# Spreading the value rows of a linear recurrence by DMA copies instead of selection matmuls

## The reference, cut to what matters

```
def step(s, rkvw):                                  # per head: s is 16 x 16 (i, j)
    r_t, k_t, v_t, w_t = rkvw
    bonus = jnp.exp(u + k_t)[..., :, None] * v_t[..., None, :]
    o_t = jnp.einsum('bhi,bhij->bhj', r_t, s + bonus)
    s = jnp.exp(w_t)[..., None] * s + k_t[..., :, None] * v_t[..., None, :]
    return (s, o_t)
```

## Time and profile before

| | |
|---|---|
| three runs | 2797.94, 2774.63, 2772.53 us; median 2774.63 us |
| profiled execution | 2782.58 us, span 2780.8 us |
| busy: PE, weight load, DVE, ACT, POOL | 2181.0 (78%), 1573.9 (57%), 1731.5 (62%), 917.0 (33%), 597.4 (21%) us |
| mean granted clock of TensorE | 0.845 |
| DMA | 34.34 MB in all, queue share 3.8% of 16 engines' span |

### The profile page before, as it was taken

How to read it: one execution, slowest core, us unless ns; L and a number is a source line. 1 busy time by engine, 2 the same in 40 slices (tenths; PEclk the granted TensorE clock), 3 DMA queues, 4 the chain that set the end, 5 groups by cost and what they waited for, 6 DMA issues and landing times. The chain is left out here.

```text
span 2780.8 us, 30306 instructions
## 1 busy us (share of the span) xinstructions
PE 2181.0 (78%) x10060; PEld 1573.9 (57%) x10060; DVE 1731.5 (62%) x3123; ACT 917.0 (33%) x2186; POOL 597.4 (21%) x357
## 2 busy tenths in 40 slices
PE   0885996796787698688678769965519999999998
PEld 0683574474465457447446645742117777777775
DVE  3335686578668668657866866866726554555544
ACT  0342452343344245234334424531004222222232
POOL 0000133033223213303322321331421011110110
PEclk9756897878888789788888878977559999999999
DMA  4000000000000000000000000000022000000000
GB/s 127 1 1 8 1 1 8 8 1 8 9 1 1 16 1 1 8 9 1 8 9 1 1 16 1 1 1 8 0 61 69 16 13 4 15 15 15 15 0 16
DMA packets 32435, 34.34 MB, mean 12 GB/s; under 512 B 4512, under 2 KB 31200, under 8 KB 31968
## 3 DMA queue, kind: packets, MB, share of 16 engines
q1 hardware_dynamic: 32288, 32.43, 3.8%
HBM read 24.04 MB, written 8.39 MB: 12 GB/s over the span
## 5 line engine op out<-in xcount | busy, mean ns | idle before, releaser
L563 DVE TENSOR_TENSOR_SCAN s_buf<-r_work,kvb 128x512 f32<-128x512 f32 x256 | 337.3, 1320 | 0.0
L719 ACT ACTIVATE probs<-bank,nmx 128x256 f32<-128x256 f32 (+1 forms) x512 | 224.4, 445 | 265.8 <-DVE nmx L425 265.5
L990 PEld LDWEIGHTS bank<-v_tok,pt 128*128 128x128 f32 x1792 | 265.3, 218 | 14.9 <-issue 3.4
L990 PE MATMUL bank<-v_tok,pt 128*128 128x16 f32 x1792 | 252.3, 272 | 2.2 <-DVE work L449 2.2
L552 DVE TENSOR_TENSOR kvb<-r_work,bank 128x512 f32<-128x512 f32 x256 | 174.3, 683 | 115.8 <-PE bank L1089 110.2
L661 POOL TENSOR_TENSOR r_work<-s_buf,r_work 128x512 f32<-128x512 f32 x128 | 157.7, 1232 | 335.0 <-DVE s_buf L563 335.0
L1544 PE MATMUL mbank<-m_xh,w_hi 128*128 128x512 f32 x544 | 228.6, 420 | 0.4 <-issue 0.3
L1352 DVE TENSOR_TENSOR hl<-hf,hh 128x512 fp32r<-128x512 f32 x136 | 94.0, 691 | 200.0 <-ACT hh L1459 199.5
L1544 PE MATMUL mbank<-m_xl,w_hi 128*128 128x512 f32 x544 | 215.5, 396 | 0.0
L1544 PE MATMUL mbank<-m_xh,w_lo 128*128 128x512 f32 x544 | 215.5, 396 | 0.0
L661 POOL TENSOR_TENSOR p_buf<-s_buf,r_work 128x512 f32<-128x512 f32 x128 | 151.4, 1183 | 291.0 <-DVE s_buf L563 284.4
(11 more groups left out here) (247 smaller groups left out, 4515.0 us busy)
## 6 DMA issues: line engine op xcount, KB each, us to landing
w_raw<-in_w SPq DMA_DIRECT2D x17, 256.0 KB, 2.7
x_new<-in_x SPq DMA_DIRECT2D x8, 512.0 KB, 3.5
x_after_rwkv<-x_b SPq DMA_DIRECT2D x8, 512.0 KB, 3.3
m_x_tok<-x_after_rwkv SPq DMA_DIRECT2D x8, 512.0 KB, 3.9
out<-m_x_tok SPq DMA_DIRECT2D x8, 512.0 KB, 2.9
w_raw<-in_w2e SPq DMA_DIRECT2D x17, 128.0 KB, 2.6
work<-in_w SPq DMA_DIRECT2D x2, 1024.0 KB
wrk<-in_wrk SPq DMA_DIRECT2D x1, 1024.0 KB
```

The lines of the kernel that those rows point to most:

```text
L563: V.tensor_tensor_scan(s_buf[:, n % 2, 1:S + 1], dec[:, n // HD, :], kvb[:, n % 2, :], 0.0, ALU.mult, ALU.add).then_inc(sem["state"], 1)
L719: ins = A(probs[:, i, h * w:h * w + w], bank[n % 2][:, h * w:h * w + w], ACT.Exp, bias=nmx[:, n, h:h + 1], accum_out=rsum[:, i, 2 * p + h: ...
L990: ins = T.matmul(A3[:, 32 * i + 16 * h:32 * i + 16 * h + 16], pt[:, m % 2, (h * len(blocks) + c) * P:(h * len(blocks) + c + 1) * P], v_tok ...
```

## The change

The values stay float32 in one SBUF tile `v_f`; `v_hi`, `v_lo`, `sel_v`, its loads and cast, and the spreading matmuls are gone. SP issues one DMA for each step, 32 in a batch, from the 8 rows of `v_f` onto the 128 rows of one of four slots of `v_bc`: each row of 2 KB is read 16 times. The DMA of step n waits until `kv(n-4)` has freed its slot. `kv(n)` now waits for its DMA, reads both inputs from SBUF, and writes into PSUM bank R0 or R1; the scan reads that bank instead of `kvb`.

```diff
+VSLOTS = 4
...
-        v_hi = sb("v_hi", [P, NK, S], F32R)
-        v_lo = sb("v_lo", [P, NK, S], F32R)
-        kvb = sb("kvb", [P, 2, S])
+        v_f = sb("v_f", [P, NK, S])
+        v_bc = sb("v_bc", [P, VSLOTS, S])
...
-            sel_rows = t["c_selv"].rearrange("(h j) n -> j h n", j=HD)
-            for j in range(HD):
-                load(raw[8 * j:8 * j + 8, 4096:6144], sel_rows[j])
...
+            def spread_v(b):
+
+                for n in range(N_SCAN):
+                    g, j, slot = n // HD, row_of(n), n % VSLOTS
+                    if n == 0:
+                        sp.wait_ge(sem["v_f"], at(b, "v_f", 2))
+                    if n >= VSLOTS:
+                        sp.wait_ge(sem["kv"], at(b, "kv", n - VSLOTS + 1))
+                    sp.dma_start(v_bc[:, slot, :], bc(v_f[8 * j:8 * j + 8, g, :].unsqueeze(1), 8, HD, S)
+                                 ).then_inc(sem[f"v_bc{slot}"], 16)
+
             next_x(0)
             with sp.Fori(1, B - 1) as b:
+                spread_v(b - 1)
                 next_x(b)
                 store(b - 1)
+            spread_v(B - 2)
             store(B - 2)
+            spread_v(B - 1)
             store(B - 1)
...
-            V.tensor_copy(sel_v[:].rearrange("p a m -> p (a m)"), raw[:, 4096:6144])
...
-                    ins = V.tensor_tensor(v_lo[:, g, :], vf[:, g, :], v_hi[:, g, :].bitcast(F32), ALU.subtract)
-                ins.then_inc(sem["v_lo"], 1)
...
                 def kv(n):
-                    ve.wait_ge(sem["v_bc"], at(b, "v_bc", n + 1))
+                    landed = f"v_bc{n % VSLOTS}"
+                    ve.wait_ge(sem[landed], at(b, landed, 16 * (n // VSLOTS + 1)))
                     if n >= 2:
                         ve.wait_ge(sem["state"], at(b, "state", n - 1))
-                    V.tensor_tensor(kvb[:, n % 2, :], kf[:, n // HD, :], RB[n % 2][:], ALU.mult).then_inc(sem["kv"], 1)
+                    if n == 1:
+                        ve.wait_ge(sem["bonus"], at(b, "bonus", 1))
+                    V.tensor_tensor(RB[n % 2][:], kf[:, n // HD, :], v_bc[:, n % VSLOTS, :], ALU.mult).then_inc(sem["kv"], 1)
...
-                        V.tensor_tensor_scan(s_buf[:, n % 2, 1:S + 1], dec[:, n // HD, :], kvb[:, n % 2, :], 0.0, ALU.mult, ALU.add
+                        V.tensor_tensor_scan(s_buf[:, n % 2, 1:S + 1], dec[:, n // HD, :], RB[n % 2][:], 0.0, ALU.mult, ALU.add
...
-                    A(v_hi[:, g, :], RB[(2 + g) % 3][:], ACT.Copy)
-                    A(vf[:, g, :], RB[(2 + g) % 3][:], ACT.Copy).then_inc(sem["v_f"], 1)
+                    A(v_f[:, g, :], RB[(2 + g) % 3][:], ACT.Copy).then_inc(sem["v_f"], 1)
...
-                def spread_v(n):
-                    g, j = n // HD, row_of(n)
-                    if n >= 2:
-                        pe.wait_ge(sem["kv"], at(b, "kv", n - 1))
-                    T.matmul(RB[n % 2][:], sel_v[:, j, :], v_hi[:, g, :], start=True, stop=False)
-                    T.matmul(RB[n % 2][:], sel_v[:, j, :], v_lo[:, g, :], start=False, stop=True).then_inc(sem["v_bc"], 1)
-
-                pe.wait_ge(sem["v_lo"], at(b, "v_lo", 1))
-                spread_v(0)
-                pe.wait_ge(sem["bonus"], at(b, "bonus", 1))
-                spread_v(1)
...
-                    if n + 2 < N_SCAN:
-                        spread_v(n + 2)
```

More of the change, by code:

```diff
@@ L38 @@
     f_lo=1, h_ps=NF, g_hi=NF, g_lo=NF, f_y=NF, fy_sb=2, fy_tok=1,
-    r_var=2, r_rstd=2, r_normed=NT, r_turned=NK, r_xt=NK, mix=8, proj=8, v_f=2, v_lo=1, k_f=2, dec=2, decay=1, r_f=2,
-    rb=1, bonus_ps=1, bonus=1, v_bc=2 * HD, kv=2 * HD, state=2 * HD, rs=2 * HD, summed=8, o_sb=2, o_tok=1, o_diff=1, o_sq=1,
+    r_var=2, r_rstd=2, r_normed=NT, r_turned=NK, r_xt=NK, mix=8, proj=8, v_f=2, k_f=2, dec=2, decay=1, r_f=2,
+    rb=1, bonus_ps=1, bonus=1, v_bc0=128, v_bc1=128, v_bc2=128, v_bc3=128, kv=2 * HD, state=2 * HD, rs=2 * HD, summed=8, o_sb=2, o_tok=1, o_diff=1, o_sq=1,
     o_var=1, o_rstd=1, o_norm=1, o_back=1, o_aff=2, y_in=1, w_ps=1, x_final=1, x_out=16, own_b=3, own_c=6, x_kept=1,
@@ L135, in mid_token_layers @@
         headones = sb("headones", [P, P])
-        sel_v = sb("sel_v", [P, HD, P], F32R)
         sel_qk = sb("sel_qk", [P, PAIRS, 4, P], F32R)
@@ L527, in rwkv_head @@
                     yield f"rmix{w}"
-                vf, kf, ek, dec, rf = (r_work[:, i:i + 2, :] for i in (0, 2, 4, 6, 8))
-                for g in range(2):
-                    ve.wait_ge(sem["v_f"], at(b, "v_f", g + 1))
-                    ins = V.tensor_tensor(v_lo[:, g, :], vf[:, g, :], v_hi[:, g, :].bitcast(F32), ALU.subtract)
-                ins.then_inc(sem["v_lo"], 1)
+                kf, ek, dec, rf = (r_work[:, i:i + 2, :] for i in (2, 4, 6, 8))
                 yield "rproj0"
@@ L543, in rwkv_head @@
                 for g, src in enumerate((R1, R2)):
-                    ins = V.tensor_tensor(o_f[:, g, :], vf[:, g, :], src[:], ALU.mult)
+                    ins = V.tensor_tensor(o_f[:, g, :], v_f[:, g, :], src[:], ALU.mult)
                 ins.then_inc(sem["bonus"], 1)
```

## The result

| | before | after |
|---|---|---|
| median of 4 runs | 2779.39 us | 2875.57 us |
| profiled execution | 2782.58 us | 2874.54 us, span 2872.7 |
| mean granted clock | 0.845 | 0.792 |
| product L552 (now L560), mean ns | 683 | 920 |
| scan L563 (now L571), mean ns | 1320 | 1210 |

After to before is 1.0318, 95% interval 1.0244 to 1.0393: slower by 3.2%, where the forecast was 9%, but inside its range of 2745 to 3105 us.

A forecast was written before the change was run, and what follows sets the result against it. The prediction took DVE to bound the scan phase before, and the copies, at 4.8 us each, after: 2782.6 + 192 (woven batches) + 66 (last batch) - 10 (setup) = 3031, or 3023 us by the median; range 2745 to 3105 us.

The forecast's parts named there:

- a tenth of it lost to PE: Woven scan phase before the change: DVE's, with 12.2 us in 11 waits for PE's spreading matmul.
- A copy alone: Service time T of one 256 KB copy from 8 neighbouring rows: 4.8 us, half of 110 GB/s; ends 1.2 and 4.8.
- T = 4.8 for every copy: Woven batches: copies land every 4.8 us, copy 28 at 122.2 us against 94.8; +27.4 us each, +192 over 7.
- Rival 3: Copies at T = 3.9 us: woven batches +5 us each, last batch +40, total 2847 or 2839 us; chance 0.10.
- the wide range: Total time, 8 in 10: 2745 to 3105 us, made to take in rival 3 and rival 1.
- rival 1: Copies hidden, product collides with POOL: last-batch steps 2.9 us, +18; woven batches -2 each; 2777 or 2769 us; chance 0.17.
- What the change frees is then worth nothing: Woven batches: PE's 30.0 us, the 12.2 us of waits and scan-POOL collisions all lie under the copy wait.
- The last batch: Last batch, recurrence alone: product 31 at 136.6 us after product 0, against 71.0; +66 us.
- The setup: Start of the kernel: without the loads and cast of `sel_v`, -10 us; ends -1 and -11.
- Operands in PSUM: DVE product writing PSUM and scan reading it: 0 extra for both, at most 0.1 us a step, under the copy.
- Rival 2: Copies hidden, product beats POOL: woven batches gain 14 us, last-batch steps 1.96 us; 2663 or 2655 us; 0.13 with rival 4.
- Rival 4: Idler PE gets a lower clock, returning up to 12 us a woven batch of rival 2's gain; 2747 or 2739; 0.13 together.

The follow-up runs named there:

- experiment 2: Changed kernel without all copies but the first four, product's second input read from the PSUM bank it writes: 2734.9 us, 0.989 of before.
- experiment 4: Changed kernel, same computation, with source rows taken in the order 0, 64, 32, 96 instead of 0, 32, 64, 96: 2806.4 us, 1.015 of before.
- experiment 9: Changed kernel with every copy reading 8 neighbouring rows among rows 0 to 63 only, so values of other channels: 2974.3 us, 1.073 of before.
- experiment 3: Changed kernel with each copy's 8 source rows 4 apart instead of neighbouring, so values of other heads: 2808.8 us, 1.017 of before.
- experiment 10: Experiment 1 with one more wait, always already met, ahead of every product: 2810.6 us, 1.014 of before.
- experiment 1: Changed kernel without all copies but the first four of the first batch; products reread those four slots without waiting: 2777.8 us, 1.004 of before.
- experiment 7: Changed kernel, whole computation, with source rows stored 4 apart and product n+2 directly behind scan n: 2745.9 us, 0.989 of before.
- experiment 5: Experiment 4 with two more 512-column matmuls in each attention step, their output overwritten: 2802.3 us, 1.011 of before.
- experiment 8: Experiment 7 with two more 512-column matmuls in each attention step: 2733.4 us, 0.986 of before.

## Why the prediction was right, and where it was wrong

**What bounds the kernel: right for the copies, wrong for PE.** DVE's own steps and waits set the pace of the scan phase, and a supplier slower than they are is felt at once. But "a tenth of it lost to PE" was no reserve: with the 12.2 us of waits gone, DVE waits for attention's matmuls instead (experiment 2).

**A copy alone: right.** Half the rate of the two groups that `sel_v`'s loads showed, 4.8 us, is what one copy takes: 51 to 53 GB/s. "Reading should suffer there as writing does" held. The figure itself owes something to luck. The 110 GB/s give the whole stretch to `sel_v`, but 199 GB/s over 10 us are 1.99 MB, and `sel_v` has 1.05 of them. With the other 0.94 MB at 373 GB/s the same working gives 3.5 us a copy, an estimate from the earlier trace rows, where 4.9 was measured. The Trainium skill, "SBUF — State Buffer" (Door 1: The DMA port swizzle), has partition bit 5 leave the port unchanged, and bit 6 and bits 4 to 2 change it; experiments 4 and 9 agree, 9.9 and 236.3 us of waits, but neither separates the page's ports from other groupings of the same rows.

**T = 4.8 for every copy: this step failed.** "copy 28 is 24 copies later: 7.0 + 24 x 4.8" took the copies as strictly one behind the other, although the working of T itself had read from the earlier trace rows that successive transfers on different groups are served together. The order of rows, 0, 32, 64, 96, was in the code, and half of the successors are on other groups. From product 4, at 1983.5 us, to product 31, at 2088.6, the real mean is 105.1 / 27 = 3.9 us. By the prediction's own 203 copies that is 0.9 x 203 = 183 us less: 2848 instead of 3031. Rival 3 had this T and this time (2847), but only as two halves that don't slow each other fully, not from the order of the rows, and with one chance in ten. The forecast's own range, T from 4.4 to 5.2 or 2942 to 3104 us, misses the measured 2876; it lies in the wide range because that was stretched to take in rivals 1 and 3.

**"What the change frees is then worth nothing": right, but it hid a cost.** At T = 3.9 a woven batch should grow by 5 us (rival 3's working), counting copies alone. It grew by 11.3, and that is the second thing that the sum missed. The 6.3 us over, 44 in seven batches, less the 17.7 us by which the first batch is shorter, are the 27 us between rival 3's 2847 and the measured 2874.5. The prediction had collisions of product and POOL, but only inside rival 1, as if the copies' waits would cover them. They don't: the wait of a woven batch is in pieces (12 waits, 16.0 us, in 778.8 to 903.5), and between them DVE is the bound. Product 0 to 28 of the third woven batch, before and then after, and the waits after:

```profile
789.10:883.90 94.80, 83.93 (x540) 68.84 (x541) 77.71 (x109) 48.37 (x164) 30.82 (x27) 0.91 0.00 1
```

```profile
778.80:881.50 102.70, 85.36 (x465) 69.32 (x473) 82.36 (x109) 47.65 (x163) 31.42 (x27) 0.72 0.44 66
```

```profile
DVE bank L560 <- DMA v_bc<-v_f: 16.0, 12, 2.5
```

The stretch is 7.9 us longer. DVE is 4.6 us longer busy (its product takes 920 instead of 683 ns there, its scan less than before) and waits 3.8 us longer for values, 16.0 instead of 12.2; its other waits are the same 4 to 5 us. So in this stretch the part above rival 3's 5 us is the collisions. Other batches at a clock of 0.63 to 0.68 took up to 111.3 us for it, with longer waits for attention's matmuls; how much of the batches' mean the lower clock makes isn't settled.

**The last batch:** forecast +66, measured +42, against rival 3's +40 at T = 3.9; that too is the size of T.

**The setup: right.** Forecast -10, measured -10.3. Operands in PSUM: right too. Product 701 instead of 687 ns, scan 1211 instead of 1219.

**The rivals,** once copies were fast: rival 1's step of 2.9 us in the last batch is experiments 3, 4 and 10 (2.8 to 3.0), but its woven batches took 5.0 us more than before, not 2 less. Rival 2's step of 1.96 us is experiments 1, 2 and 7 (1.9), but of its 14 us a woven batch only 0.4 to 2.2 came. Rival 4, the same with PE's saving given back to the clock, had 2739 to 2747 us; experiments 2 and 7 measured 2735 and 2746, with the clock in 7 at 0.73 where it had been 0.84. Its mechanism is what experiment 2 shows: the waits move to attention's matmuls, and the stretch takes 95.7 us at 0.70 and 84.8 at 0.84. Raising the clock with added matmuls (5, 8) brought 1.5 and 2.8 us a batch, since they take time of PE too.

## What to carry to other kernels

A DMA that spreads a few rows over many is priced by where its source rows lie, and a sequence of them by how each one's rows lie to its successor's; work out the mean over the real order, not the worst of one. When an input of a DVE instruction moves from PSUM to SBUF, find the POOL instruction that is released beside it: whichever starts first makes the other wait, and the order of a single wait on DVE can turn that around. When a change takes a wait away, look for the next wait behind it on the same engine; here DVE's wait for one group of matmuls became a wait for another, and PE's lower clock took back most of what was freed.

## What was not expected of the hardware

- The granted clock can undo nearly a whole saving: 57 matmuls fewer, PE as long busy (92.1 and 93.0 us of about 120 and 116). In one execution of experiment 2 the same stretch took 95.7 us at 0.70 and 84.8 at 0.84.
- The collision between DVE and POOL is decided by hundredths: 0.04 us ahead, the product takes 0.70 us; 0.02 to 0.03 us behind, 1.62 or 1.79.
- Two orders of the same 256 copies differ by 146 us of waits (experiment 4).
- The first batch, without any of the changed work, differed by 18 us between kernels with the same setup, with a granted clock of 0.81 or 0.69.
